# One wait of the recurrence moved, and the norms' scaling set fourteen units behind centring, with the reciprocal in two halves

## What is computed

```python
x = x + L0_conv(ln_c(x))      # norm over channels, then four sweeps (rows down, up; columns right, left)
t = t + L0_ffn(ln_t(t))       # tokens; norm over channels; 32 experts, 8 tokens each, gathered and scattered
x = x + L1_conv(ln_c(x))      # as the first
t = t + L1_ffn(ln_t(t))       # Wx = t @ W.T, batch norm, then a recurrence over all 3600 tokens:
                              #   y = sigmoid(wx_t + y @ V.T)
```

## Time and profile before

| | us |
|---|---|
| median of 3 runs | 4286.70 |
| lowest, highest | 4286.59, 4288.07 |
| the profiled execution, its own time | 4284.66 |
| the span of its profile | 4282.9 |

### The profile page before, as it was taken

One profiled execution on the slowest core, in us unless ns is written; L12 is line 12 of the kernel. 1 busy time (PEld: TensorE's weight loads), 2 busy tenths in 40 slices (PEclk: granted clock), 3 DMA queues, 4 the chain that ended last, 5 costly groups with the idle time before them and its releaser, 6 DMA issues.

```text
span 4282.9 us, 138615 instructions
## 1 busy us (share of the span) xinstructions
PE 4142.7 (97%) x57258; PEld 3149.5 (74%) x57258; DVE 1331.6 (31%) x2528; ACT 2059.6 (48%) x8972; POOL 119.8 (3%) x243
## 2 busy tenths in 40 slices
PE   8999999998889999999998899999999999999999
PEld 2899999994452899999994366666666666666666
DVE  4555533334556655533335600000000000000000
ACT  5002344445545002334444366666666666666666
POOL 1000000000010000000000000000000000000000
PEclk9999999999999999999999899999999999999999
DMA  5000000003348000000006300000000000000000
GB/s 145 11 0 0 0 0 0 0 0 115 94 116 253 23 0 0 0 0 0 0 0 170 100 15 21 22 15 22 21 15 22 18 19 21 15 21 22 15 21 18
DMA packets 178458, 144.78 MB, mean 34 GB/s; under 512 B 110910, under 2 KB 177502, under 8 KB 178014
## 3 DMA queue, kind: packets, MB, share of 16 engines
q1 hardware_dynamic: 177486, 137.58, 12.2%
q10 hardware_dynamic: 528, 0.63, 0.1%
HBM read 79.19 MB, written 58.98 MB: 32 GB/s over the span
## 4 chain that ended last, share of the span: by engine, by line
PE 94%; DVE 3%; issue 1%; ACT 1%; DMA 0%; SPq 0%; POOL 0%; DVEq 0%; ACTq 0%; POOLq 0%
PE ps L945 23%; PE ps L795 21%; PE ps L773 18%; PE ps L864 16%; PE ps L859 3%; PE ps L577 2%; PE ps L569 1%; PE ps L744 1%; PE ps L588 1%; PE ps L598 1%; PE ps L612 1%; DVE rstd L1177 1%; PE ps L836 1%; PE ps L711 1%; PE ps L642 1%
## 5 line engine op out<-in xcount | busy, mean ns | idle before, releaser
L1157 ACT ACTIVATE xl<-ps 64x8 f32<-64x8 f32 x7200 | 1221.1, 171 | 613.0 <-PE ps L945 611.7
L945 PEld LDWEIGHTS ps<-xl,vt 65*32 65x32 f32 x28800 | 1042.9, 108 | 632.0 <-ACT xl L1157 392.7
L945 PE MATMUL ps<-xl,vt 65*32 65x8 f32 x28800 | 1448.8, 183 | 26.5
L864 PE MATMUL ps<-idle 128*32 128x256 bf16 (+1 forms) x5886 | 1370.0, 273 | 3.6 <-POOL ident L490 3.6
L795 PE MATMUL ps<-xl,taps 128*128 128x128 f32 (+2 forms) x7880 | 914.0, 279 | 4.7 <-DVE xl L1349 4.7
L795 PEld LDWEIGHTS ps<-xl,taps 128*128 128x128 f32 x7880 | 913.6, 191 | 5.4 <-issue 5.3
L773 PE MATMUL ps<-split 128*128 128x400 f32 x4140 | 780.9, 351 | 12.5 <-DVE split L1344 12.5
L773 PEld LDWEIGHTS ps<-split 128*128 128x128 f32 x4140 | 778.8, 190 | 16.2 <-issue 14.8
L1437 DVE TENSOR_TENSOR xl<-xl 64x320 f32<-64x320 f32 x180 | 125.1, 695 | 1710.0 <-ACT xl L1157 1710.0
L1012 ACT ACTIVATE img<-xl 128x144 f32 x788 | 365.7, 464 | 549.2 <-DVE xl L1326 549.2
L864 PEld LDWEIGHTS ps<-idle 128*32 128x32 bf16 x5886 | 583.3, 99 | 24.7 <-issue 10.9
(11 more groups left out here) (154 smaller groups left out, 1666.2 us busy)
## 6 DMA issues: line engine op xcount, KB each, us to landing
ring<-in_x_dram SPq DMA_DIRECT2D x144, 200.0 KB, 3.7
x_dram<-sums SPq DMA_DIRECT2D x144, 200.0 KB, 3.3
t_dram<-sums SPq DMA_DIRECT2D x72, 200.0 KB, 3.7
ring<-t_dram SPq DMA_DIRECT2D x72, 200.0 KB, 3.9
ring<-x_dram SPq DMA_DIRECT2D x72, 200.0 KB, 3.7
xl<-x_dram SPq DMA_DIRECT2D x45, 320.0 KB, 4.7
out_dram<-xl SPq DMA_DIRECT2D x45, 320.0 KB, 3.5
img<-in_L_ffn_weight_dram SPq DMA_DIRECT2D x4, 512.0 KB
```

What stands on the lines that cost most here:

```text
L864: pe.matmul(PS[bank][0:32, 0:n], idle[:, 0:32], idle[:, 0:n], start=True, stop=True)
L945: last = pe.matmul(PS[2 * s + h][c * 32:(c + 1) * 32, t * HB:(t + 1) * HB], vt[:, c * 32:(c + 1) * 32], prev, start=False, stop=True, skip ...
L1157: act.activation(yb[0:64, s, h * HB:(h + 1) * HB, t], PS[2 * s + h][0:64, t * HB:(t + 1) * HB], ACT.Sigmoid).then_inc(step_y[h], 1)
```

## The change

Four edits, of which the second and third act in the three pipelined norms, and the third also in norm 1.

- In the recurrence the wait for `added` stands before the last piece of `fill_input` (t = 7), not behind it.
- LAG is 14 (NCH + 5) where it was 12, KEPT 15 where it was 13; `wsc` moves out of the way of the longer ring in `xl`.
- The reciprocal is taken in two halves of 200 columns (INVERSES), each counted on `inverse`; in the pipelined norms the first half stands at iteration n = 11, 20, 29, 38, the second one iteration later, each behind that iteration's scale.
- The 14 idle products before the last group are gone in norms 0, 2 and 3, and stay in norm 1.

```diff
-        wsc = [xl[:, 5760 + h * 64:5824 + h * 64] for h in range(2)]
+        wsc = [xl[:, 6272 + h * 64:6336 + h * 64] for h in range(2)]
...
-        LAG = NCH + 3
+        LAG = NCH + 5
+        INVERSES = 2
...
-        KEPT = NCH + 4
+        KEPT = NCH + 6
...
                     if i == 1 or n == LAST:
                         pe.wait_ge(st.kept, 2 * (n + NCH))
+                    if i == 1:
                         for _ in range(14):
                             keep_clock(pe, 512, MOVE[1])
-                    pe.wait_ge(st.inverse, g + 1)
+                    pe.wait_ge(st.inverse, INVERSES * (g + 1))
...
                         pe.wait_ge(st.kept, 2 * UNITS)
-                        for _ in range(14):
-                            keep_clock(pe, 512, SPARE)
                     elif i == 0 and n == 0:
                         pe.wait_ge(spread_ready, 1)
-                    pe.wait_ge(st.inverse, g + 1)
+                    pe.wait_ge(st.inverse, INVERSES * (g + 1))
...
                             if t == 0:
                                 pe.wait_ge(staged, seg + 2)
+                            elif t == 2 * FILLS - 1:
+                                pe.wait_ge(added, seg + 2)
                             last = fill_input(pe, 1 - s, t)
                             if t == 2 * FILLS - 1:
                                 last.then_inc(filled, 1)
-                                pe.wait_ge(added, seg + 2)
...
-        def invert(dve, i, g):
-            r0 = rstd[:, (g % 2) * CH:(g % 2 + 1) * CH]
+        def invert(dve, i, g, part):
+            n = CH // INVERSES
+            a = (g % 2) * CH + part * n
             dve.wait_ge(ln[i].std, g + 1)
-            dve.reciprocal(r0, r0).then_inc(ln[i].inverse, 1)
+            dve.reciprocal(rstd[:, a:a + n], rstd[:, a:a + n]).then_inc(ln[i].inverse, 1)
...
-                    invert(dve, i, g)
+                    for part in range(INVERSES):
+                        invert(dve, i, g, part)
...
-                if 3 <= n < UNITS + 3 and n % NCH == 2:
-                    invert(dve, i, n // NCH - 1)
+                if NCH <= n < UNITS + NCH and 2 <= n % NCH < 2 + INVERSES:
+                    invert(dve, i, n // NCH - 1, n % NCH - 2)
```

## The result

The changed kernel takes 4259.3 us (median of 4 runs, 4257.07 to 4264.86) against 4286.65 before: ratio 0.9938, 95% interval 0.992 to 0.9955. On a second chip, where the kernel before took 4291.0, it took 4258.3, ratio 0.9924 (0.9911 to 0.9938). The forecast of 4254 is 5 us too low: the time lies 0.3 above the forecast's own range, which ends at 4259, and inside the wider one that counts the clock rival in, to 4267. The profiled execution took 4264.86, the slowest of the four; its span is 4263.1, 19.8 under that of before.

What follows compares the result with a forecast made beforehand. The prediction took PE's chain of waits, chiefly the recurrence, as the bound. It summed -14.6 - 11.8 - 5.5 - 0.8 + 0.3 = -32.4 us, giving 4252.3 profiled, 4254 as median; range 4245 to 4259, to 4267 with the clock rival.

Steps and rivals of the forecast that it cites:

- the clock rival: The first rival: clock still falls after the first reciprocals of norms 0 and 2; 4263 us, chance 0.17.
- Recurrence, -14.6: Part 1: moving `added` off PE's late product removes 0.082 us from 179 late steps, one per segment; 14.6 us gained.
- the late row: Recurrence profile row at t = 7, read as a second, long fulfilled wait making the step 0.08 us late.
- Norm 0, -11.8: Part 2: earlier first spread, clock, boundary stops and tail in norm 0, summed as -5.8 - 3.4 - 3.1 + 0.5.
- iteration 14: The iteration that begins with the first spread; forecast 5.8 us earlier in norm 0, 2.6 in norm 3.
- the clock and both stops: Norm 0: iterations 14 and 15 at full clock save 3.35 us; two later boundary stops of 1.55 go, 3.1.
- the tail: A norm's end, with two more units left to scale; forecast +0.5 us in norm 0, +1.5 norm 2, +4.0 norm 3.
- Norm 2, -5.5: Part 3: first spread 5.1 us earlier, at about 1323.7; later boundaries save 1.9, tail costs 1.5.
- The later boundaries: Norm 2: PE's stops of 1.57 us at later groups partly go, 0.95 each, 1.9 us gained.
- Norm 3, -0.8: Part 4: iteration 14 2.6 us earlier, two boundary stops of 1.08 gone (-2.2), two more units in the tail (+4.0).
- Norm 1, +0.3: Part 5: norm 1 isn't pipelined, so both reciprocal halves stand on its path; 0.07 us more, four times.
- The last rival: Slower: half clock through units 14 to 35 of norms 0 and 2; 4328 us if all 44, chance 0.02.

Runs made afterwards that it cites:

- e1: Experiment 1: the kernel before with only the recurrence's wait for `added` moved; 4276.6 us, ratio 0.9969.
- e8: Experiment 5: the kernel before with both waits left on half 1's product at t = 7, `step_y` written ahead of `added`; 4276.06 us, ratio 0.9963.
- e2: Experiment 2: the changed kernel with a second, long fulfilled wait for `added`, written after `step_y`, on half 1's product at t = 10; 4259.36 us.
- e6: The changed kernel with lag 12 and the reciprocal whole again; 4279.67 us, ratio 0.9976.
- the repetition: The changed kernel itself measured again, beside runs with rebuilt tails; 4258.27 us, ratio 0.9924.
- experiment 6 (e4): The changed kernel with the 14 idle products ahead of the last group back in norms 0, 2 and 3; 4271.23 us, ratio 0.9958.
- experiment 7, e5: The changed kernel with the reciprocal whole again (INVERSES = 1), lag 14 and no idle products; 4270.4 us, ratio 0.9958.
- e9: The changed kernel with norms 0 and 2's last half reciprocals two iterations earlier and last spreads starting in free banks; 4262.09 us, ratio 0.9932.
- e12: On top of e9, four idle products after each of iterations 36 to 39 of norms 0 and 2; 4255.74 us, ratio 0.9916.

## Why the prediction was right, and where it was not

**Recurrence, -14.6: -14.2**, shown by experiments 1 and 5. The cause was put wrongly: "PE's late product keeps one wait" is not what gains, since with two in the other order it is as fast. The step that failed is the reading of the late row as the price of a second wait. What costs is the late wait, `step_y`, as an instruction of its own: 1832.80 and 1832.81 where it stands alone, 1818.51 and 1818.10 where `added` does. The number came out because it was read off the late row itself, whatever its cause. The Trainium skill, Perfetto Trace Analysis, section "Tensor Engine Instruction (MATMUL, LD_WEIGHTS)", which I set aside on that row, has the sequencer go on once an instruction is in its wait queue; the trace agrees for the wait that stays on the product (experiments 2 and 5). The Trainium skill, Perfetto Trace Analysis, section "Identifying Dependency Chains", says that an instruction that waits for several engines may have instructions for the other waits put ahead of it; L941's 180 are these.

**Norm 0, -11.8: -10.8** against the profiled execution of before, by the terms forecast, counted from the norm's start: iteration 14 5.2 earlier (forecast 5.8), the clock and both stops 6.6 (6.45), the tail +1.0 (+0.5). But experiments 1 and 5 (e1, e8), with the old norm 0, took 108.4 and 111.1, and against the mean of the three, 110.6, the five traces of the changed code, mean 101.6, stand at -8.9. The term for the clock, 3.35, is most of that: in e1 the same stop of 1.64 was not followed by half clock. It is real all the same. With a lag of 12 the clock fell behind the first reciprocal in three traces of four (before, e6, e8), and with 14 in none of ten.

**Norm 2, -5.5: -1.2** in that trace, -3.5 in the repetition; against the mean of the three traces of the old code, 135.5, the five of the changed code, mean 130.4, stand at -5.1. The step that failed in the profiled execution is "PE centres two units meanwhile; first spread at about 1323.7": it came at 1321.0 in a norm that began 5.5 earlier, 2.8 late, at half clock. That is the first rival, in norm 2 and not in norm 0: ahead of that spread the clock was low in four of the five traces (not in e2). I had overlooked that PE then waits for the square root (1.65) and a total (0.89) instead of the reciprocal. The later boundaries gave 1.3 (forecast 1.9). The tail grew by 2.35, to 19.1 from 16.8, for +1.5; the old code's own took 18.3 in e1. That the means agree with the forecast is luck in part: e1 and e8 had 13.7 and 16.9 us at half clock between the first spread and the last variance sums of norm 2, where the trace that the forecast was read from had 6.8 and the change has none.

**Norm 3, -0.8: 0.0** (165.15 to 165.12), by -2.0 for iteration 14 (forecast -2.6), -2.0 for the boundaries (-2.2) and +4.0 for the tail (+4.0). But it took 168.06 and 168.05 in two of the five traces of the changed code, nearly all of it ahead of the first spread.

**Norm 1, +0.3:** the term was the right one and is tiny: two halves end to end take 2.67 (995.45 to 998.12) against 2.65. The +5.1 of this trace is none of the change's: the same code took 304.67 in experiment 6 (e4). In the profiled execution, 12.6 above the 4252.3 of its own scale, this scatter makes 4.8 and norm 2 4.3. On the second chip the gain was the 32.7 forecast (4286.7 to 4254); but there the kernel before stood 4.4 higher, so that this agreement is partly luck.

**Idle products.** I took their removal as a help in the tails of norms 0 and 2, in part of their time only. With the longer lag they are worth more (experiment 6, e4), because nothing covers them any more: before, the last reciprocal ran beside them. And the halves, which I priced by the spreads' stops, are not needed for these, since the lag alone takes them away; they earn some 10 us through what DVE does between them (experiment 7, e5).

## What to carry to other kernels

Where an instruction needs two waits, write the one that ends late first, if, as here, the one written last becomes the instruction of its own; look in the chain of waits for steps with more "issue" than their neighbours. When a long instruction sits in an engine's list between short ones that another engine waits for, price the delay of everything queued behind it, not only that of its own result. A gain that rests on the clock staying up should be counted over several executions before it is believed.

## What the hardware showed

In the tails, where centring has ended and PE issues spreads alone (with the idle products ahead of some of them in the kernels that have these), the granted clock fell to half in norms 0 and 2 of every profile taken, though PE was busy 14.81 of 16 us (e9). In e12 it fell with no stop ahead of it: PE was busy all of the time from 88.0 to 102.0, with spreads alone from 97.73 on, and the clock went down at 102.3. Sixteen idle products among the spreads put this off (0.76 for 0.52) and did not prevent it. The last rival expected half clock through the pipelined norms; between the first spread and the last variance sums of norms 0 and 2 none of the five traces of the change has any. What about the spreads brings the clock down no run here shows.
